# A graph layer on one Trainium2 core: the first edge product moved ahead of the transposes and sums on TensorE, and ScalarE's e_r and tanh moved with it

## What is computed

```
h   = max(layernorm(x), 0)                       # x: 100000 x 128, f32
for each of 50000 edges (src, dst, type of 4):
    m = relu([h[src], h[dst]] @ W1[type] + b1[type]) @ W2[type] + b2[type]
agg = segment_sum(m, dst)                        # edges come sorted by dst
gi  = agg @ W_ih.T + b_ih ;  gh = h @ W_hh.T + b_hh
r = sigmoid(gi_r + gh_r) ; z = sigmoid(gi_z + gh_z)
n = tanh(gi_n + r * gh_n)
out = x + (1 - z) * n + z * h
```

## Time and profile before

| what | value |
|---|---|
| median of 3 runs | 1777.2 us (1776.45 to 1779.61) |
| the profiled execution: its own time, its span | 1777.92 us, 1776.0 us |
| busy over the span: TensorE, its weight loads, VectorE, ScalarE, GpSimd | 92%, 80%, 90%, 82%, 70% |
| chain that ended last, TensorE's share | 87% |
| granted TensorE clock, mean over the span | 0.995 |

### The profile page before, as it was taken

The page is one execution under the profiler, slowest core; times in us unless marked ns, Lnnn a source line. Parts: engine busy times, 40 slices in busy tenths (PEclk is TensorE's granted clock), DMA queues, the critical chain, the costliest instruction groups (busy, mean ns, idle before and its releaser), DMA issues.

```text
span 1776.0 us, 43100 instructions
## 1 busy us (share of the span) xinstructions
PE 1625.5 (92%) x10182; PEld 1428.5 (80%) x10182; DVE 1597.8 (90%) x4186; ACT 1457.6 (82%) x3401; POOL 1240.2 (70%) x1982
## 2 busy tenths in 40 slices
PE   0216799999999999999999999999999999999998
PEld 0215688888888888888888888888888888888886
DVE  8597599999999999999999999999999999999886
ACT  0025689898998999999989999999999998999895
POOL 4777778777777777777776766667667666676420
PEclk9999899999999999999999999999999999999999
DMA  2214577777777777777777777777777777777653
GB/s 72 49 46 125 151 204 199 200 200 198 201 204 193 205 195 200 198 193 202 195 199 197 196 198 199 194 202 194 200 197 194 201 194 199 194 197 197 182 140 98
DMA packets 477071, 319.72 MB, mean 180 GB/s; under 512 B 106705, under 2 KB 463009, under 8 KB 476962
## 3 DMA queue, kind: packets, MB, share of 16 engines
q10 hardware_dynamic: 261792, 156.12, 29.1%
q1 hardware_dynamic: 185730, 106.99, 25.6%
q0 software_dynamic: 29440, 55.47, 12.6%
HBM read 211.65 MB, written 106.72 MB: 179 GB/s over the span
## 4 chain that ended last, share of the span: by engine, by line
PE 87%; ACT 1%; issue 1%; DVE 0%; POOL 0%; DVEq 0%; ACTq 0%; POOLq 0%
PE bank L1335 16%; PE bank L1337 15%; PE bank L1336 15%; PE bank L1415 10%; PE bank L1427 5%; PE bank L1426 5%; PE bank L1443 5%; PE bank L1405 5%; PE bank L1453 5%; PE bank L1397 5%; PE bank L1439 1%; ACT n_zc L1288 0%; POOL e_x L580 0%; DVE n_sel L1074 0%; ACT e_h L1180 0%
## 5 line engine op out<-in xcount | busy, mean ns | idle before, releaser
L580 POOL DMA_INDIRECT e_x<-in_x,rows_now x816 | 852.4, 1045 | 237.0 <-issue 217.8
L1180 ACT ACTIVATE e_h<-e_x,shift,rstd 128x128 f32<-128x128 f32 x816 | 355.4, 485 | 117.3 <-DVE shift L1051 94.3
L1197 ACT ACTIVATE n_h<-n_x,shift,rstd 128x128 f32<-128x128 f32 x784 | 385.5, 492 | 0.1
L1335 PE MATMUL bank<-n_h_hi,whh_hi 128*128 128x512 f32 x588 | 247.9, 422 | 2.4 <-ACT n_zc L1288 2.1
L1335 PE MATMUL bank<-n_a_hi,wih_hi 128*128 128x512 f32 x588 | 248.8, 423 | 0.9 <-DVE bank L1086 0.9
L1074 DVE TENSOR_SCALAR n_sel<-iota,n_rel 128x256 fp32r<-128x256 f32 x784 | 239.2, 366 | 8.7 <-POOL n_rel L631 6.7
L1415 PE MATMUL bank<-n_sel,n_win 128*128 128x256 f32 x1568 | 234.4, 292 | 10.9 <-DVE n_sel L1074 10.9
L1337 PE MATMUL bank<-n_a_hi,wih_lo 128*128 128x512 f32 x588 | 232.4, 395 | 0.0
L1336 PE MATMUL bank<-n_h_lo,whh_hi 128*128 128x512 f32 x588 | 232.4, 395 | 0.0
L1337 PE MATMUL bank<-n_h_hi,whh_lo 128*128 128x512 f32 x588 | 232.2, 395 | 0.0
L1336 PE MATMUL bank<-n_a_lo,wih_hi 128*128 128x512 f32 x588 | 231.9, 394 | 0.0
(11 more groups left out here) (179 smaller groups left out, 3767.4 us busy)
## 6 DMA issues: line engine op xcount, KB each, us to landing
n_win<-messages SPq DMA_DIRECT2D x1568, 64.2 KB
messages<-e_msg ACTq DMA_DIRECT2D x204, 257.0 KB, 3.1
n_x<-in_x ACTq DMA_DIRECT2D x195, 256.0 KB
out<-n_out ACTq DMA_DIRECT2D x195, 256.0 KB, 2.3
e_x<-in_x,rows_now POOLq DMA_INDIRECT x816
rows_now<-lists SPq DMA_DIRECT2D x204, 2.0 KB, 3.1
lists<-picks,list_rows POOLq DMA_INDIRECT x72
w<-in_W SPq DMA_DIRECT2D x1, 512.0 KB, 5.0
```

The lines of the kernel that those rows point to most:

```text
L580: G.indirect_dma_start(e_x[:, s, 2 * end + t, :], None, x, bass.IndirectOffsetOnAxis(ap=rows_now[:, s, t, end:end + 1], axis=0)).then_inc( ...
L1180: last = A.activation(e_h[:, s % 2, k, :], e_x[:, s, k, :], ACT.Relu, scale=rstd[:, slot, col + k:col + k + 1], bias=shift[:, slot, col + ...
L1197: last = A.activation(n_h[:, s % 2, cols], n_x[:, s, cols], ACT.Relu, scale=rstd[:, slot, col + 4 + k:col + 5 + k], bias=shift[:, slot, co ...
L1335: T.matmul(o, w_hi, v_hi, start=start, stop=False, skip_group_check=onto)
```

## The change

On TensorE the block of the first edge layer (the wait for `e_evaced` and `e_low`, eight instructions, `e_hid`) goes from behind the message sums to behind the n gate's h half. On ScalarE the ReLU `e_r`, which waits for `e_hid`, goes from behind the second tile of `n_h` to ahead of `e_ht`; and the tanh `n_n` with the load of x goes ahead of the third tile of `n_h`. No instruction is added or taken away, and VectorE's, GpSimd's and SyncE's programs stay as they are.

```diff
@@ ScalarE's step
                 store_messages(i, m)
                 normalise_edges(i, m, (2, 3))
-                q, s = i - 8, (m - 8) % 2
-                if within(q, UNITS):
-                    act.wait_ge(e_turned, q + 1)
...
-                    A.activation(e_ht[:, s, :], bank[BE0][:], ACT.Copy).then_inc(e_evaced, 1)
...
-                    A.activation(n_h_hi[:, s, :], bank[BT[s]][:], ACT.Copy).then_inc(n_hhi, 1)
-                normalise_nodes(i, m, (0,))
...
-                    A.activation(n_a_hi[:, s, :], bank[BA][:], ACT.Copy).then_inc(n_ahi, 1)
-                store_out(i, m)
-                normalise_nodes(i, m, (1,))
                 q, s = i - 9, (m - 9) % 2
                 if within(q, UNITS):
                     act.wait_ge(e_hid, q + 1)
...
                         last = A.activation(e_r[:, s, cols], bank[BE1][:, cols], ACT.Relu, bias=b1_cols[:, kind:kind + 1])
                     last.then_inc(e_relued, 1)
+                q, s = i - 8, (m - 8) % 2
+                if within(q, UNITS):
+                    act.wait_ge(e_turned, q + 1)
...
+                    A.activation(e_ht[:, s, :], bank[BE0][:], ACT.Copy).then_inc(e_evaced, 1)
...
+                    A.activation(n_h_hi[:, s, :], bank[BT[s]][:], ACT.Copy).then_inc(n_hhi, 1)
+                normalise_nodes(i, m, (0,))
...
+                    A.activation(n_a_hi[:, s, :], bank[BA][:], ACT.Copy).then_inc(n_ahi, 1)
+                store_out(i, m)
+                normalise_nodes(i, m, (1,))
                 g, s = i - LAG, (m - LAG) % 2
-                normalise_nodes(i, m, (2,))
                 if within(g, NG):
                     act.wait_ge(n_gate_in, g + 1)
...
                     A.activation(n_n[:, s, :], bank[BIN][:], ACT.Tanh, bias=bih[:, 2:3]).then_inc(n_ned, 1)
                 load_x(i, m)
+                normalise_nodes(i, m, (2,))
@@ TensorE's step
                     gate(BHN, 2, s, "h").then_inc(n_gate_hn, 1)
+                q, s = i - 9, (m - 9) % 2
+                if within(q, UNITS):
+                    pe.wait_ge(e_evaced, q + 1)
+                    if due(q):
+                        pe.wait_ge(e_low, q)
+                    for t in range(2):
...
+                    last.then_inc(e_hid, 1)
...
                     last.then_inc(n_summed, 1)
-                q, s = i - 9, (m - 9) % 2
-                if within(q, UNITS):
-                    pe.wait_ge(e_evaced, q + 1)
...
-                    last.then_inc(e_hid, 1)
```

More of the change, by code:

```diff
@@ L1247, in step @@
                 normalise_edges(i, m, (2, 3))
+                q, s = i - 9, (m - 9) % 2
+                if within(q, UNITS):
+                    act.wait_ge(e_hid, q + 1)
+                    if due(q - 1):
+                        act.wait_ge(e_messaged, q - 1)
+                    for t in range(2):
+                        cols = slice(t * P, (t + 1) * P)
+                        kind = 2 * ((m - 9) % 2) + t
+                        last = A.activation(e_r[:, s, cols], bank[BE1][:, cols], ACT.Relu, bias=b1_cols[:, kind:kind + 1])
+                    last.then_inc(e_relued, 1)
                 q, s = i - 8, (m - 8) % 2
@@ L1390, in step @@
                     gate(BHN, 2, s, "h").then_inc(n_gate_hn, 1)
+                q, s = i - 9, (m - 9) % 2
+                if within(q, UNITS):
+                    pe.wait_ge(e_evaced, q + 1)
+                    if due(q):
+                        pe.wait_ge(e_low, q)
+                    for t in range(2):
+                        o = bank[BE1][:, t * P:(t + 1) * P]
+                        kind = 2 * ((m - 9) % 2) + t
+                        T.matmul(o, w1[:, kind, 0, :], e_ht[:, s, t * P:(t + 1) * P], start=True, stop=False)
+                        last = T.matmul(o, w1[:, kind, 1, :], e_ht[:, s, (2 + t) * P:(3 + t) * P], start=False, stop=True)
+                    last.then_inc(e_hid, 1)
                 q, s = i - 8, (m - 8) % 2
```

## The result

The changed kernel takes 1786.0 us (median of 6 runs, 1785.9 to 1786.8) against 1777.1 us (6 runs, 1776.5 to 1779.6): the ratio is 1.0049, interval 1.0036 to 1.0062. It is 8.9 us, half a per cent, slower. The forecast was 1780.0 us and no change, with a range up to 1785.0: the time lies 1 us outside. The profiled execution took 1786.0 us with a span of 1784.1.

What follows compares the result with a forecast made beforehand. TensorE, back to back, was taken to bound the kernel, with nothing spare at `n_out` in fourth steps. +4.4 - 0.5 - 1.1 = +2.8 us on 1777.92 gave 1780.7, less 0.7 for the median: 1780.0 us, range 1774.0 to 1785.0.

Steps and rivals of the forecast that it cites:

- What bounds the kernel: Whole kernel: TensorE's matmuls run back to back, VectorE has 0.52 us idle in a step, nothing spare at `n_out` every fourth step.
- TensorE's move: Edge-layer block behind the h half: its eight instructions cost the same, one operand-type change fewer per step, 0.5 us gained.
- ScalarE's move: `e_r` ahead of `e_ht`, tanh earlier: `n_a_hi` ends at 912.24, ScalarE is free 0.23 us before `n_zc`; priced at nothing.
- VectorE's price: VectorE's queue from `n_a_lo` to `n_out`: late in 49 fourth steps at 0.09 us each, 4.4 us lost, bounds 0 and 9.8.
- The spare that I took off: Fourth steps other than the one read: assumed 0.06 us to spare, which reduced the priced lateness to 0.09 us.
- The slip of 0.15: Fourth steps: `n_e` starts at 914.61 instead of 914.46, 0.15 us late, with `n_out` and the h half behind it.
- The rule cited from the Trainium skill: VectorE, `n_d` to `n_e`: a semaphore between consecutive Vector instructions costs nothing extra, making the loss 0; the prediction's rows spoke against it.
- The start: First r gate: begins 2.1 us earlier, near 197, worth half at 1.2 GHz: 1.1 us gained, bounds 0 and 2.1.
- the bound of 3.1: Kernel's start: upper limit of the gain, 2.1 us and 1 more if the clock rises sooner.
- Rival 1: Slower, chance 0.35: VectorE's chain slips 0.15 to 0.20 us in each fourth step, run 5.8 to 8.2 us longer, 1783.0 to 1785.4.
- its other terms, -1.6: Gains set against the fourth steps' loss: 0.5 us from operand types and 1.1 us from the earlier first r gate.
- the dearer part of rival 1: Slow end of the forecast range, set at 1785.0 us, within the slower case's 1783.0 to 1785.4.

## Why the prediction was wrong

**What bounds the kernel** held: TensorE back to back, VectorE with half a microsecond to spare in a step, and the tight place at `n_out`.

**TensorE's move** held. Its eight instructions cost the same. I had 0.5 gained by one change of operand type less. The three traces with the new order and no wait for `n_out` take 1434.9 to 1435.1 us for steps 22 to 201, the three with the old order 1435.5 to 1435.8: 0.4 to 0.9 gained. That it comes from the operand types was argued, and no run shows it.

**ScalarE's move** held. In the rows of after, counted from the r gate's start at 1101.34, `e_r` starts at 3.26 (forecast 909.82 - 906.54 = 3.28), `n_a_hi` at 5.12 (5.12), `n_n` at 6.05 (5.98), and `n_zc` is released by the z gate. One thing was missed: `n_h_hi` and `n_a_hi` now run 0.61 us, against 0.58 in the earlier trace rows (0.59 in the median of that trace).

**VectorE's price was the step that failed.** The mechanism is the one written down, in the places written down: `n_a_lo` at 5.76 behind the r gate (5.73), `n_d` at 7.33 (7.29), `n_e` by 0.10 behind `n_d`'s end (0.09). The size is where it went wrong: "I take other such steps to have the difference, 0.06, to spare, and price the slip at 0.09". Measured over the trace, the second matmul of the h half, behind which all follows, comes 0.16 us later than in an undisturbed step in one half of the fourth steps, and 0.26 in the other half: 0.21 on average. In the 44 of them between steps 22 and 201 that is 9.1 us; their length grew by 8.8.

The spare that I took off was right: in the trace of before, `n_out` ends at 1.26 us behind the r gate in the median step of that kind, and TensorE can take it until 1.32. The slip of 0.15 was too small. With `n_a_hi`'s longer run `n_e` starts 8.11 behind the r gate, where it had been 7.92 (forecast 8.07): 0.19 late. And such a step now lasts 8.01 us and not 8.03, so the next r gate comes 0.02 sooner and `n_out` is 0.21 later against it, which less 0.05 is the 0.16. That this lies near the 0.15 written down ahead of the discount is chance.

The 0.26 belongs to the steps behind the top of the loop of eight, a kind that the prediction did not tell apart; the rows that I read were of the other half. In those `half_var` starts 0.18 behind the cast (1108.39 and 1108.57 in after); at the top of the loop it is 0.29, before the change too (0.28), and why isn't shown:

```profile
947.09 0.20 DVE L1111 CAST e_msg<-rows_now 128x2 f32<-128x2 int32 x1
947.38 0.18 DVE L1043 TENSOR_SCALAR half_var<-bn 128x32 f32<-128x32 f32 x1
```

**The rule cited from the Trainium skill**, page "VectorE: DVE Perf Modes", section "The DRAIN you can't avoid" (a semaphore between two consecutive Vector instructions costs nothing extra), would have made the term 0. This case's trace does not agree: `n_d` and the linked `n_e` start 1109.45 - 1108.67 = 0.78 us apart, while `n_e` and `n_out` of the same size, unlinked, start 0.61 apart in the run with `root` moved. This difference of 0.17 is near the size of the whole slip. No run took the wait itself away.

**The start** was mis-sized: 1.1 for 2.5. The order's own share, 1.6 to 1.9, is nearer the 2.1 than the half of it that I took for the clock; and the clock rose 4 us sooner, which the prediction had only in its bounds. My doubt was about what granted clock the earlier work would meet, and the bound of 3.1 held it. This error made the forecast too slow, not too fast.

**The exit from the loop** was no term at all: +2.5 us, of which 1.5 are the clock's fall in step 204 and 0.3 the wait for `n_out` in two fourth steps; the rest is the balance of ScalarE's stalls, whose cause stays open. Steps 202 and 203 of the kernel before, at 9.8 and 9.1 us instead of 8.0, were there to be seen.

**The chances.** Rival 1 had 0.35 and is what happened in the steady steps, at the top of its "0.15 to 0.20" or just above. That its 5.8 to 8.2 us also hold the whole span's 8.1 is luck: its other terms, -1.6, came out near -0.6, because the exit's +2.5, which it did not have, cancelled the start's -2.5. The range stopped at "the dearer part of rival 1" and left its upper end out, although 49 x 0.20 = 9.8 stood in the text as a bound.

## What to carry to other kernels

Take the slack of a saturated engine's suppliers for each kind of step (here four, and eight with the loop's top), since lateness is paid where the spare is least: one step read gave a slip of 0.15, and the two kinds of step that pay had 0.21 and 0.31. Look at the steps behind a loop's end too, and at what the clock does behind the waits there. A moved block delays what it passes: look for small instructions that stand in the queue between there and the release, for a single one of 0.18 us, put where its engine waits anyway, was worth as much as the whole change lost. And an engine that produces in order needs its consumer reordered too: TensorE's move alone cost 80 us.

## What the runs showed of the hardware

- **Behind a late release TensorE loses more than its first matmul shows.** In the tight step the weight load of the h half starts 0.05 us behind `n_out` and the first matmul at once, but the second matmul follows at 0.33 us (1110.88 to 1111.21) and not at 0.23 (1111.21 to 1111.44). Over the traces with such waits the second matmul starts 0.39 to 0.40 us behind the end of `n_out`, whenever that ends late: 1.47 gives 1.87 behind the r gate's start, 1.58 gives 1.97. Undisturbed it starts at 1.71. So an `n_out` that ends by 1.32 costs nothing, and one that ends at 1.38, as in the run with small instructions everywhere, delays the second matmul by 0.06 although the first still starts on time (1.48). The r gate, whose matmuls wait for `n_zc` in every step, shows such a first distance too: 1109.35 to 1109.66, 0.31.
- **ScalarE's copies of PSUM take 0.61 us in the new order and 0.59 in the old** (medians of `n_a_hi`; the step shown has 0.61 at 1106.46, has 0.58), with the same shapes. Why wasn't tried.
- **The granted clock at the start differs between executions whose start is the same**: it rises at 201.7 us in the kernel before and at 197.7 in the one with the old start and the new steady part, worth 0.6 us at the r gate of step 22. Both begin the first r gate at 199.1.
- **TensorE's clock can fall behind a wait in the middle of a kernel.** Behind idle times of 2.2 to 2.3 us in step 203 the granted clock fell to half in three traces (at 1685.5 us in the changed kernel), which cost 1.5 us in the next step; behind 2.2 us in the run with the tanh back and 2.5 us in the one with the old start it did not fall. What decides isn't shown.
- The stalls of ScalarE behind the loop's exit stay open. Steps 201 to 205 take 42.7 to 45.6 us over the thirteen traces, a spread as large as a third of what this change took.
